# The Mamba stage of a decoder kernel: silu whole on ScalarE, the residual added by TensorE, five read-outs on GpSimd in other steps

## The reference

```
residual = hidden + residual
h   = layernorm(residual) * norm_w + norm_b
xin, z = split(h @ in_proj.T)
xc  = silu(causal_conv(xin) + conv_b)
dtr, B, C = split(xc @ x_proj.T)
dt  = softplus(dtr @ dt_proj.T + dt_b)
state = exp(dt * A) * state + (dt * xc) * B      # for each token and each of 16 states
y   = sum over states(state * C) + xc * D
hidden = (y * silu(z)) @ out_proj.T
```

## Time and profile before

| | us |
|---|---|
| median of 3 runs | 9063.85 |
| lowest and highest | 9046.51, 9091.64 |
| the profiled execution | 9078.0 |
| its span | 9076.0 |

### The profile page before, as it was taken

One profiled execution on the slowest core, in us unless ns is written; L12 is line 12 of the kernel. 1 busy time (PEld: TensorE's weight loads), 2 busy tenths in 40 slices (PEclk: granted clock), 3 DMA queues, 4 the chain that ended last, 5 costly groups with the idle time before them and its releaser, 6 DMA issues. The chain is left out here.

```text
span 9076.0 us, 93651 instructions
## 1 busy us (share of the span) xinstructions
PE 6563.1 (72%) x25895; PEld 3515.8 (39%) x25895; DVE 6900.3 (76%) x14998; ACT 4377.4 (48%) x8762; POOL 4905.9 (54%) x2837
## 2 busy tenths in 40 slices
PE   5888888887888888887887455555555777777755
PEld 2333333333333333333554333333333445455532
DVE  5999999999999999996554666666666776666657
ACT  3555555555555555554553222222223666666633
POOL 4888888888888788885442333333322333333310
PEclk8989898899988998898887777777755888988865
DMA  4333343333333333332101444444421000000001
GB/s 173 140 146 156 138 159 140 146 143 149 153 139 155 143 148 140 147 152 79 28 24 44 135 126 130 130 130 132 129 64 33 10 9 9 9 9 9 9 28 36
DMA packets 368247, 902.20 MB, mean 99 GB/s; under 512 B 28191, under 2 KB 263068, under 8 KB 301500
## 3 DMA queue, kind: packets, MB, share of 16 engines
q1 hardware_dynamic: 325116, 688.97, 20.2%
q0 software_dynamic: 42880, 210.80, 8.1%
HBM read 856.34 MB, written 56.77 MB: 101 GB/s over the span
## 5 line engine op out<-in xcount | busy, mean ns | idle before, releaser
L380 POOL TENSOR_TENSOR mb_dBu<-mb_dtu,mb_rows_b 128x1024 f32<-128x1024 f32 x1027 | 2406.3, 2361 | 357.1 <-DVE mb_bank L394 184.4
L394 DVE TENSOR_TENSOR_SCAN mb_bank<-mb_bank,mb_dBu 128x1024 f32<-128x1024 f32 x704 | 1611.9, 2290 | 71.7 <-PEq L63 51.0
L434 PE MATMUL mb_bank<-mb_hcd,ident 128*128 128x512 f32 x2560 | 1264.2, 621 | 70.7 <-DVE mb_hcd L408 70.7
L365 ACT ACTIVATE mb_bank<-mb_dt,mb_a_neg 128x508 f32<-128x508 f32 x2050 | 1310.7, 670 | 0.8
L434 PE MATMUL mb_bank<-mb_hcp,ident 128*128 128x512 f32 x1280 | 795.6, 755 | 372.1 <-POOL mb_hcp L417 372.1
L1563 POOL DMA_INDIRECT ex_rows<-in_ex_table,ex_idx x536 | 525.8, 981 | 960.7 <-PE ex_bank L1648 705.0
L417 POOL TENSOR_TENSOR mb_hcp<-mb_hs,mb_rows_c 128x1024 f32<-128x1024 f32 x320 | 752.8, 2353 | 356.7 <-DVE mb_hs L394 353.6
L408 DVE TENSOR_TENSOR mb_hcd<-mb_bank,mb_rows_c 128x1024 f32<-128x1024 f32 x704 | 861.7, 1224 | 31.4
L434 PEld LDWEIGHTS mb_bank<-mb_hcd,ident 128*128 128x128 f32 x2560 | 499.9, 202 | 783.1 <-issue 587.3
L394 DVE TENSOR_TENSOR_SCAN mb_hs<-mb_bank,mb_dBu 128x1024 f32<-128x1024 f32 x320 | 730.8, 2284 | 41.1 <-ACT mb_bank L365 41.1
L434 PEld LDWEIGHTS mb_bank<-mb_hcp,ident 128*128 128x128 f32 x1280 | 283.8, 235 | 822.1 <-POOL mb_hcp L417 498.9
(11 more groups left out here) (366 smaller groups left out, 13873.6 us busy)
## 6 DMA issues: line engine op xcount, KB each, us to landing
mb_rows_b<-bc_rows SPq DMA_DIRECT2D x259, 1024.0 KB, 7.6
mb_rows_c<-bc_rows SPq DMA_DIRECT2D x258, 1024.0 KB, 6.8
stream<-mb_r_post SPq DMA_DIRECT2D x69, 256.0 KB, 2.3
mb_r_tok<-stream SPq DMA_DIRECT2D x67, 256.0 KB, 2.8
mb_r_post<-stream SPq DMA_DIRECT2D x65, 256.0 KB, 2.8
ex_rows<-in_ex_table,ex_idx POOLq DMA_INDIRECT x536
ex_x_tok<-stream SPq DMA_DIRECT2D x17, 256.0 KB, 2.9
tj_x_tok<-stream SPq DMA_DIRECT2D x17, 256.0 KB, 3.0
```

What stands on the lines that cost most here:

```text
L365: e = nc.scalar.activation(da_of(n)[:, c * GB:(c + 1) * GB, 1:], dt[q][:, c].rearrange("p (b t) -> p b t", b=GB)[:, :, 1:], ACT.Exp, scale ...
L380: nc.gpsimd.tensor_tensor(by_c(dBu[m % RING][:]), by_c(chains(dtu[q][:])), over_c(rows_b[:, n]), ALU.mult).then_inc(s["mb_dbu"], 1)
L394: nc.vector.tensor_tensor_scan(flat(to), flat(da_of(n)), flat(dBu[n % RING][:]), 0.0, ALU.mult, ALU.add).then_inc(s["mb_scan"], 1)
L434: m = nc.tensor.matmul(bank[:, B_Y + c], ident[:], part[:, c * GB:(c + 1) * GB], start=False, stop=False)
```

## The change

ACT makes both silus by its own Silu function: one instruction for each half of the convolution (both now at n = 3) and one for the whole of z. L215, L219 and L294 go, u is no longer doubled, and the scalings of w_x and w_out go. The polynomial's Square goes to an SBUF tile `sq`, so `x_psum` stays and `pe_dt` is made once. The residual's old rows are fetched to a tile of their own, `r_old`; PE multiplies them with the identity as the first product of the group in bank M1, the out projection adds to it, and ACT copies the sum to r_post (at n = 1, behind the exponentials for step 2); DVE's add goes. POOL's read-outs are those of steps 1, 4, 7, 10, 13.

```diff
-ON_POOL = (2, 4, 8, 10, 12)
+ON_POOL = (1, 4, 7, 10, 13)
...
             def act_conv(self, act, c):
                 act.wait_ge(s["mb_conv"], c + 1)
-                nc.scalar.activation(th[:, c], bank[:, M0 + c], ACT.Tanh, scale=0.5, bias=conv_bh[:, c:c + 1]).then_inc(s["mb_tanh"], 1)
-                act.wait_ge(s["mb_tanh"], c + 1)
-                nc.scalar.activation(th[:, c], th[:, c], ACT.Identity, bias=1.0).then_inc(s["mb_th"], 1)
-
-            def dve_conv(self, dve, c):
...
+                nc.scalar.activation(u[self.q][:, c], bank[:, M0 + c], ACT.Silu, bias=conv_b[:, c:c + 1]).then_inc(s["mb_u"], 1)
...
-                nc.scalar.activation(x_psum, ey[:], ACT.Square, scale=THIRD, bias=poly_at[:, 0:1]).then_inc(s["mb_sq"], 1)
+                nc.scalar.activation(sq[:], ey[:], ACT.Square, scale=THIRD, bias=poly_at[:, 0:1]).then_inc(s["mb_sq"], 1)
...
             def dve_dt(self, dve):
                 dve.wait_ge(s["mb_log"], 1)
-                dve.wait_ge(s["mb_dtp"], 2)
...
             def act_z(self, act):
-                for c in range(CH):
-                    act.wait_ge(s["mb_z"], c + 1)
-                    nc.scalar.activation(zth[:, c], bank[:, M0 + c], ACT.Tanh, scale=0.5).then_inc(s["mb_zth"], 1)
-
-            def dve_z(self, dve):
...
+                act.wait_ge(s["mb_z"], CH)
+                nc.scalar.activation(zg[self.q][:], x_psum, ACT.Silu).then_inc(s["mb_zg"], 1)
...
             def pe_out(self, pe):
+                pe.wait_ge(s["mb_rp"], 16)
+                nc.tensor.matmul(bank[:, M1], ident[:], r_old[:].rearrange("p b d -> p (b d)"), start=True, stop=False)
                 pe.wait_ge(s["mb_yg"], 1)
                 for b in range(GB):
                     for c in range(CH):
                         m = nc.tensor.matmul(bank[:, M1, b * D:(b + 1) * D], yg[:, c, b * SEQ:(b + 1) * SEQ],
-                                             w_out[:, c], start=(c == 0), stop=(c == CH - 1))
+                                             w_out[:, c], start=False, stop=(b == GB - 1 and c == CH - 1))
                 m.then_inc(s["mb_out"], 1)
...
-            def dve_add(self, dve):
...
+            def act_new(self, act):
+                act.wait_ge(s["mb_out"], 1)
+                nc.scalar.activation(r_post[:].rearrange("p b d -> p (b d)"), bank[:, M1], ACT.Copy).then_inc(s["mb_new"], 1)
...
                         if n == 1:
-                            ahead.act_conv(act, 0)
+                            behind.act_new(act)
                         if n == 3:
-                            ahead.act_conv(act, 1)
+                            for c in range(CH):
+                                ahead.act_conv(act, c)
...
-                        if n == 10:
-                            ahead.pe_dt(pe, True)
```

More of the change, by code:

```diff
@@ L105, in mamba_stage @@
         h_ch = sb("h_ch", [P, GB, KW])
-        th, zth = sb("th", [P, CH, TOK]), sb("zth", [P, CH, TOK])
         xp = sb("xp", [2 * DS + DR + 1, TOK])
-        ab, ey, ln1, small = (sb(n, [P, CH, TOK]) for n in ("ab", "ey", "ln1", "small"))
-        dt, dtu, u2, zg = (pair(n, [P, CH, TOK]) for n in ("dt", "dtu", "u2", "zg"))
+        ab, ey, sq, ln1, small = (sb(n, [P, CH, TOK]) for n in ("ab", "ey", "sq", "ln1", "small"))
+        dt, dtu, u, zg = (pair(n, [P, CH, TOK]) for n in ("dt", "dtu", "u", "zg"))
         rows_b, rows_c = sb("rows_b", [P, DS, TOK]), sb("rows_c", [P, DS, TOK])
@@ L115, in mamba_stage @@
         hcp = pair("hcp", [P, CH * GB, SEQ])
-        yg, r_post = sb("yg", [P, CH, TOK]), sb("r_post", [P, GB, D])
+        yg, r_old, r_post = sb("yg", [P, CH, TOK]), sb("r_old", [P, GB, D]), sb("r_post", [P, GB, D])
         NW, NB, CB, DD, AL = 0, 1, 2, 2 + CH, 2 + 2 * CH
@@ L152, in mamba_stage @@
             "res", "rp", "store", "rows", "b0", "b1", "b2", "b3", "c0", "c1", "c2", "c3",
-            "stats", "norm", "xh", "tr", "h", "conv", "tanh", "th", "u", "xp", "xps", "dtp", "abs", "ey", "sq", "small", "ln", "poly", "log", "dt", "dtu", "z", "zth", "zg",
+            "stats", "norm", "xh", "tr", "h", "conv", "u", "xp", "xps", "dtp", "abs", "ey", "sq", "small", "ln", "poly", "log", "dt", "dtu", "z", "zg",
             "dbu", "da", "scan", "hcd", "hcp", "sumd", "sump", "y", "yg", "out", "new", "raw", "weights", "wb", "skip", "wo", "apos", "aneg"]])
@@ L224, in pe_x @@
                 for c in range(CH):
-                    m = nc.tensor.matmul(bank[0:2 * DS + DR, M0], w_x[:, c], u2[self.q][:, c], start=(c == 0), stop=(c == CH - 1))
+                    m = nc.tensor.matmul(bank[0:2 * DS + DR, M0], w_x[:, c], u[self.q][:, c], start=(c == 0), stop=(c == CH - 1))
                 m.then_inc(s["mb_xp"], 1)
@@ L235, in store_rows, with pe_dt @@
                 sp.wait_ge(s["mb_rows"], 16)
-            def pe_dt(self, pe, again):
-                pe.wait_ge(s["mb_log"], 1) if again else pe.wait_ge(s["mb_xps"], 1)
+            def pe_dt(self, pe):
+                pe.wait_ge(s["mb_xps"], 1)
                 for c in range(CH):
@@ L260, in dve_poly @@
                 dve.wait_ge(s["mb_sq"], 1)
-                nc.vector.scalar_tensor_tensor(out=x_psum, in0=x_psum, scalar=0.8125, in1=ey[:], op0=ALU.add,
+                nc.vector.scalar_tensor_tensor(out=sq[:], in0=sq[:], scalar=0.8125, in1=ey[:], op0=ALU.add,
                                                op1=ALU.mult).then_inc(s["mb_poly"], 1)
@@ L421, in pe_skip @@
                 for c in range(CH):
-                    nc.tensor.matmul(bank[:, B_Y + c], skip[:, c], u2[self.q][:, c], start=True, stop=False)
+                    nc.tensor.matmul(bank[:, B_Y + c], skip[:, c], u[self.q][:, c], start=True, stop=False)
             def pe_sum(self, pe, n):
@@ L517, in _ @@
                 dve_skip(dve)
-                for c in range(CH):
-                    first.dve_conv(dve, c)
                 first.dve_poly(dve)
@@ L522, in _ @@
                 first.dve_dt(dve)
-                first.dve_z(dve)
                 dve.wait_ge(s["mb_res"], 2 * 16)
@@ L546, in _ @@
                 first.pe_x(pe)
-                first.pe_dt(pe, False)
-                first.pe_dt(pe, True)
+                first.pe_dt(pe)
                 first.pe_z(pe)
@@ L643, in _ @@
                             behind.dve_gate(dve)
[L644 to L649, removed]
                         if n == 6 and shape == 0:
-                            nc.vector.tensor_scalar(w_out[:], out_raw[:], 0.25, None, ALU.mult).then_inc(s["mb_wo"], 1)
+                            nc.vector.tensor_copy(w_out[:], out_raw[:]).then_inc(s["mb_wo"], 1)
                         if n == 6 and shape == GROUPS - 2:
@@ L686, in _ @@
                         if n == 5:
-                            ahead.pe_dt(pe, False)
+                            ahead.pe_dt(pe)
                         if n == 10:
@@ L715, in _ @@
                 last.dve_gate(dve)
-                last.dve_add(dve)
+            @block.scalar
+            def _(act):
+                last.act_new(act)
             @block.tensor
```

28 lines of the change are left out of this document (7 added, 21 removed).

## The result

| | us |
|---|---|
| median of 4 runs | 9186.92 |
| lowest and highest | 9180.3, 9194.73 |
| the kernel before in the same comparison, median | 9063.97 |
| ratio, 95% interval | 1.0133 [1.0106, 1.016] |
| the profiled execution, its span | 9185.18, 9183.1 |

The change made the kernel slower by 1.3%, about 120 us; the forecast was 9085, the range 8995 to 9180. All of it lies in the Mamba stage. From the starts of the scans in the two traces, a round takes 65.28 us on average over 63 rounds, against 63.57 before, and 1.71 x 64 is 109 us; the two profiled executions are 107 apart, and what lies outside these 63 rounds takes 5071 us in both. It is taken from one profile, but it leaves the other stages out: what lies outside the 63 rounds took 5013 to 5119 us in the profiles of this document, which were taken on several chips.)

A forecast was written before the change was run, and what follows sets the result against it. TensorE's chain bounds a round's first half, GpSimd closes it: 61.8 + 0.75 x 1.4 (slow z) + 0.88 (slow starts) = 63.7, plus 0.2 tail, 63.9 against 63.6 us; +20 us, forecast 9085, range 8995 to 9180.

The forecast's parts named there:

- What bounds; the first half: Before scan 8, TensorE's chain sets the time; the identity product's 0.86 us makes this half 0.87 us longer.
- The walk: One round followed engine by engine from its first scan; GpSimd closes it at 60.95 us, giving a 61.8 us round.
- The polynomial in SBUF: VectorE's poly before scan 10 reads SBUF instead of PSUM: counted at nothing, bounds 0.1 us either way.
- The tail: TensorE's last sums after step 13: 0.2 us a round; as rival, at half clock, 9145 us in all, chance 0.28.
- The clock: TensorE starting a round at 1.2 GHz costs 1.75 us; taken for half the rounds, 0.88 us.
- its 1.4: Second half: extra round time when the z product runs at 1.2 GHz, taken for 3 of 4 rounds.
- Sum: Whole round: 63.9 us against 63.6, +0.3 a round, +20 us in all, forecast 9085.
- Silu in the table of Exp: ScalarE's Silu needs no loads of its own, so z is in time; faster rival, 9010 us, chance 0.20.
- DVE's time in full: VectorE's removed work and wait, 5.2 us a round, come through fully; rival, -330 us to 8735, chance 0.04.
- A change of table at twice its load: Each of two loads in the z branch costs 1.28 us more; rival, +164 us to 9250, chance 0.03.

The follow-up runs named there:

- polynomial: Kernel before with only the polynomial moved to SBUF and one L242; ratio 1.005, mean round 64.15 us.
- PSUM operand: Changed kernel with L253 and L260 each reading one operand from PSUM instead of sq, and an always-zero mask; ratio 0.9986, mean round 63.28 us.
- one table: Changed kernel with Relu in place of Silu in L212 and L279, so two table loads a round, not six; ratio 1.013, mean round 65.36 us.
- VectorE's add: Changed kernel with the residual added by VectorE again, without identity product and ScalarE copy; ratio 1.009, mean round 65.22 us.
- steps: Kernel before with only GpSimd's read-outs moved to steps 1, 4, 7, 10, 13; ratio 1.0103, mean round 65.04 us.
- silu: Kernel before with only ScalarE's Silu for convolution and z, VectorE losing L219 and L294; ratio 1.0078, mean round 64.70 us.
- residual: Kernel before with only the residual's identity product and ScalarE's copy; ratio 1.0053, mean round 64.63 us.
- the three with four read-outs: Four GpSimd read-outs on the changed kernel (1.0127), on the kernel before with SBUF polynomial (0.9965), and with the paying parts combined (0.9934).
- the late sums: Kernel before with the SBUF polynomial, TensorE taking GpSimd's read-outs one step later in its order; ratio 0.9921, mean round 62.45 us.

## Why the prediction was wrong

**What bounds; the first half.** Right. The walk said 8.04 for out, 14.9 for the second convolution, 27.43 for L242, 18.3 for scan 5 behind 2.4 us of wait, 30.9 for scan 8. The rows above give, from 2259.73, 8.04, 14.91, 27.44, 18.32 with 2.33 of wait, and 30.90.

**The polynomial in SBUF.** The step that failed. "Poly reads SBUF instead of PSUM, which I count at nothing (bounds 0.1 either way)": it was 1.14 + 1.13 = 2.27 us a round on VectorE, and moving the two operands to PSUM gave back 2.0 us a round (128 us over the 64). The two bounding rows (L311 and L273) have a PSUM operand each, so they could not bound an operation without one. The trace before held a row that could, had I looked for one: L455, a line of the weights' preparation with two SBUF inputs, takes 409 to 2561 ns in one and the same form, and the longest, from 3058.02 to 3060.58, ends 0.28 us after the POOL product beside it (3060.30).

```profile
L455 DVE TENSOR_TENSOR mb_w_conv<-mb_w_u,mb_conv_row x20: 409/417/2561, 61.0 to 4081.4; 128x256 f32<-128x256 f32 x20
```

The Trainium skill has the rule, in "SBUF — State Buffer", section "SBUF: two separate sides": a DVE operation with two SBUF inputs and a GpSimd operation that reads SBUF take the same port pair as an exclusive lock for the whole instruction, and the second one blocks. The traces agree, by 1.14 and 1.13 us on DVE in the changed kernel and 0.83 on POOL in the kernel before with the polynomial alone. With these 2.3 the walk gives POOL's end as 60.95 + 2.3 = 63.3 (measured 63.4); without them, in the run with the PSUM operand, it ends at 61.2. That run, the change as the prediction priced it, has a mean round of 63.28 and a ratio of 0.9986, where the forecast had 63.9 and 1.002.

**The tail.** It was a rival, with the sums behind step 13 at the half clock, and 0.2 us of the forecast. Measured it is 0.8 beyond POOL in most rounds, up to 2 in some. So forecast and rival stood on the right place; the term in the sum was mis-sized by 0.6, and the rival with this tail (9145, chance 0.28) came nearest of all the cases, without the step that failed.

**The clock.** I took half of the rounds as starting slow (0.88 us). One of 63 did: out ends at 8.03 to 8.16 in almost all. What sets it no run isolates, but the kernels sort by who ends the round. Where the sums do, so that PE works up to the barrier, 1 to 4 of 63 rounds start slow (changed, one table, PSUM operand, VectorE's add, steps, polynomial); where VectorE does, 9 to 53 (before 30, silu 53, residual 48, the three with four read-outs 9, 9 and 17). With the late sums POOL ends last, and 13 do. Z was slow in 61 rounds (3.78 us, forecast three of four), and as POOL and the sums end later anyway its 1.4 did not show.

**Sum.** 61.8 + 2.3 + 0.8 = 64.9 with z and the starts at nothing; a typical round is 65.1. The forecast had 61.8 + 1.05 + 0.88 + 0.2. The terms for z and the slow starts, 1.9 in all, did not add to the round; 2.3 and 0.6 were missing. That the measured time lies only 7 us outside the range is thus in part luck.

**Rivals.** Silu in the table of Exp: no, four loads more a round. DVE's time in full: no (and its 5.2 a round is 0.4 under its own rows, 3.4 + 2.2). A change of table at twice its load: no, L279's silu follows its load and PE's z at once.

## What to carry to other kernels

Before moving an operand from PSUM to SBUF, ask which engines' instructions will then have two inputs there, and whether GpSimd runs beside them; a bar that got longer without idle time in front of it is the sign. Where TensorE takes its work in a fixed order, put what comes late from a slow engine behind what is ready: one line of order was worth more (a ratio of 0.9921 to the kernel before, where the same kernel without it has 1.005) than the five removed VectorE operations, with which the kernel got slower. And freeing the busiest engine brings little when three engines end a round within a microsecond or two of each other: walk each of them to its end.

## What the runs showed that I had not expected

The exclusion hits small operations as well, and not only those with two SBUF inputs: L171, 128x4, with one input, takes 1155 ns in the median of the changed kernel and 170 before (L172), since it now falls in a POOL product. It ends at 2289.73, and that product, started at 2287.35, ends at 2289.70. It costs nothing here, as scan 8 waits another 0.83 us for ScalarE behind it. It comes with the steps, not with the polynomial: 1151 ns in the kernel with the steps alone, 170 in that with the polynomial alone.
Nothing stands between a table load and its function: L212's silu starts at 2272.80, 0.01 us after the load of 2271.51 ends.
The four parts alone cost 0.5, 0.5, 0.8 and 1.0%, 2.8% in sum, and together 1.3%. Two things speak to it, though no run isolates them: each alone meets an end of round at which the next engine is already late, and silu and the residual alone have more slow starts (53 and 48 of 63) than the four together (1).
